# Softplus logs in PSUM, both C products on VectorE each eighth step, and two residual adds moved to TensorE and ScalarE in a Mamba, MoE and attention kernel

## The reference, cut to what matters

```python
# x: (8, 512, 512) f32; every layer adds to the residual
x = x + mamba(layernorm(x))      # L0_attn_a, the scan stage
x = x + moe(layernorm(x))        # 64 experts, top 6 by softmax, and a shared expert
x = x + attention(layernorm(x))
x = x + moe(layernorm(x))

def mamba(x):                    # per batch of 512 positions, 512 channels, 16 states
    xz = einsum('bld,kd->blk', x, W_x)
    dt_raw, b_ssm, c_ssm = xz[..., :128], xz[..., 128:144], xz[..., 144:]
    dt = softplus(einsum('blr,dr->bld', dt_raw, W_dt) + b_dt)
    d_a = exp(dt[..., None] * -exp(A_log))
    dbx = dt[..., None] * b_ssm[:, :, None, :] * x[..., None]
    # h = d_a_t * h + dbx_t;  y_t = sum over the states of h * c_t
    return y + x * D_param
# the shared expert of the MoE layer: silu(h @ sw_gate) * (h @ sw_up) @ sw_down
```

## Time and profile before

| | |
|---|---|
| median of 3 runs | 3007.59 us (3006.03 to 3013.62) |
| profiled execution | 3010.63 us, span 3008.8 us |
| PE, DVE, POOL, ACT busy | 2720.0, 1793.9, 1528.1, 1298.4 us |

### The profile page before, as it was taken

The page is one execution under the profiler, slowest core; times in us unless marked ns, Lnnn a source line. Parts: engine busy times, 40 slices in busy tenths (PEclk is TensorE's granted clock), DMA queues, the critical chain, the costliest instruction groups (busy, mean ns, idle before and its releaser), DMA issues.

```text
span 3008.8 us, 37440 instructions
## 1 busy us (share of the span) xinstructions
PE 2720.0 (90%) x13484; PEld 1436.8 (48%) x13484; DVE 1793.9 (60%) x3787; ACT 1298.4 (43%) x2689; POOL 1528.1 (51%) x944
## 2 busy tenths in 40 slices
PE   4668889988998879999969999999899999999998
PEld 2455555545555534443335555555544444444443
DVE  5899999999999952232246666665524444222222
ACT  4557586766757411111127767666712220111111
POOL 5999999989999902222135555554400001121211
PEclk7769999998999889999989999999999999999999
DMA  5443645546454479999930000001135324899997
GB/s 189 150 168 139 204 168 171 189 136 192 164 192 162 138 295 355 396 394 392 380 109 1 29 29 29 29 29 58 47 100 196 117 74 164 307 383 338 361 334 219
DMA packets 168234, 566.13 MB, mean 188 GB/s; under 512 B 22832, under 2 KB 24752, under 8 KB 167536
## 3 DMA queue, kind: packets, MB, share of 16 engines
q1 hardware_dynamic: 149904, 521.65, 46.7%
q0 software_dynamic: 17088, 40.90, 5.9%
q10 hardware_dynamic: 1056, 1.18, 0.1%
HBM read 487.89 MB, written 75.79 MB: 187 GB/s over the span
## 4 chain that ended last, share of the span: by engine, by line
PE 54%; ACT 2%; DVE 2%; POOL 2%; issue 1%; DMA 1%; POOLq 0%; SPq 0%; DVEq 0%; ACTq 0%
PE bank L1140 10%; PE bank L1166 5%; PE bank L1078 5%; PE bank L1043 5%; PE bank L1064 5%; PE bank L1191 5%; PE bank L1248 4%; PE bank L1225 3%; PE bank L1213 2%; PE bank L1237 2%; POOL arena L1947 2%; PE bank L1123 1%; PE bank L1179 1%; ACT arena L1770 1%; PE bank L1050 1%
## 5 line engine op out<-in xcount | busy, mean ns | idle before, releaser
L1851 POOL TENSOR_TENSOR arena<-arena 128x1024 f32<-128x1024 f32 x256 | 606.3, 2369 | 6.3 <-DMA arena<-scratch_bc 3.0
L1699 ACT ACTIVATE bank<-arena 128x512 f32<-128x512 f32 x512 | 346.6, 689 | 318.9 <-DVE arena L1337 200.5
L1947 POOL TENSOR_TENSOR arena<-arena 128x2048 f32<-128x2048 f32 (+3 forms) x128 | 297.1, 2324 | 275.9 <-DVE arena L1567 275.8
L993 PE MATMUL bank<-arena 128*128 128x128 f32 x2048 | 306.3, 303 | 141.7 <-POOL arena L1857 141.6
L993 PEld LDWEIGHTS bank<-arena 128*128 128x128 f32 x2048 | 260.4, 156 | 227.7 <-POOL arena L1857 181.8
L1770 ACT ACTIVATE arena<-arena 128x256 f32<-128x256 f32 (+3 forms) x512 | 287.2, 566 | 148.9 <-DVE arena L1558 125.2
L1857 POOL TENSOR_TENSOR arena<-arena 128x512 f32<-128x512 f32 x256 | 334.2, 1306 | 21.4 <-DVE arena L1337 21.3
L1337 DVE TENSOR_TENSOR_SCAN arena<-bank,arena 128x512 f32<-128x512 f32 x256 | 310.6, 1213 | 24.8 <-POOL arena L1851 18.6
L1140 PE MATMUL bank<-arena 128*64 128x352 f32 x2048 | 322.7, 468 | 0.0
L1337 DVE TENSOR_TENSOR_SCAN bank<-bank,arena 128x512 f32<-128x512 f32 x256 | 308.4, 1205 | 0.0
L1064 PE MATMUL bank<-arena 128*128 128x512 f32 x640 | 288.3, 593 | 9.1 <-ACT arena L1726 9.1
(11 more groups left out here) (145 smaller groups left out, 4161.3 us busy)
## 6 DMA issues: line engine op xcount, KB each, us to landing
arena<-scratch_bc SPq DMA_DIRECT2D x128, 1024.0 KB, 5.4
arena<-in_w_out SPq DMA_DIRECT2D x128, 768.0 KB, 15.3
arena<-in_w_gate SPq DMA_DIRECT2D x128, 704.0 KB
arena<-in_w_up SPq DMA_DIRECT2D x128, 704.0 KB
scratch_x<-arena SPq DMA_DIRECT2D x16, 1024.0 KB, 4.5
scratch_xn<-arena SPq DMA_DIRECT2D x15, 1024.0 KB, 4.1
arena<-scratch_x SPq DMA_DIRECT2D x44, 256.0 KB, 6.0
arena<-scratch_x SPq DMA_DIRECT2D x8, 1024.0 KB, 7.5
```

The lines of the kernel that those rows point to most:

```text
L993: i = nc.tensor.matmul(y[:, t * P:(t + 1) * P], w[:, n, t * P:(t + 1) * P], p.ident, is_transpose=True, start=False, stop=g == GROUPS - 1 ...
L1699: nc.scalar.activation(bank[p.da_bank(k, n)][:, :], block_of(p.dt, b, c), ACT.Exp, scale=p.alog[:, c, state:state + 1]).then_inc(*p.decaye ...
L1851: nc.gpsimd.tensor_tensor(out=p.hb[k % HB], in0=over(block_of(p.dtx, b, c), 1, NG), in1=p.bc[k // 2 % NBC][:, 0], op=ALU.mult).then_inc(*p ...
L1947: nc.gpsimd.tensor_tensor(out=own, in0=own, in1=over(p.rden[:, k % 2, :], 2, width), op=ALU.mult).then_inc(*p.divided.up(k))
```

## The change

Softplus: `soft_ln` writes the logs of one chunk (128x512) into a bank of the small ring, and `dt_sum` adds them from there, chunk by chunk. Its steps and those of dt are moved forward by one to three. Each eighth step (k % 8 == 4) VectorE leaves the first scan in its bank too and makes both C products, and GpSimd makes none. `y_sum` begins a chunk's bank with identity times x, so that the bank holds the new residual, and `x1` is a copy by ScalarE, three steps behind. For quads 0 to 6 of the first MoE layer the down tile ends with identity times the fetched residual rows, and ScalarE copies it out; the fetch is issued a step earlier. GpSimd's small norm operations (`rstd`) stand a step later.

```diff
+BOTH_EVERY, BOTH_AT = 8, 4
-PREPARE = (("x_in", 4), ("stats_a", 7), ("stats", 8), ("rstd", 8), ("apply", 11))
-TURN_S, DTR, BC, DT = (13, 13, 14, 14), 16, 15, (21, 21, 22, 25)
-SOFT = (("soft_exp", (24, 28)), ("soft_ln", (26, 29)), ("dt_sum", (27, 30)), ("dtx", (28, 31)))
-FRONT = (("stats_a", 1), ("stats", 1), ("rstd", 1), ("apply", 3), ("xn_out", 3), ("gate", 7), ("logit", 9), ("route_max", 10), ("route_exp", 12), ("route1", 13), ("masks", 15))
+PREPARE = (("x_in", 4), ("stats_a", 7), ("stats", 8), ("rstd", 9), ("apply", 11))
+TURN_S, DTR, BC, DT = (13, 13, 14, 14), 16, 15, (19, 19, 20, 22)
+SOFT = (("soft_exp", (24, 27)), ("soft_ln", (25, 28)), ("dt_sum", (26, 29)), ("dtx", (27, 30)))
+BY_BLOCK = ("soft_ln", "dt_sum")
+FRONT = (("stats_a", 1), ("stats", 1), ("rstd", 2), ("apply", 3), ("xn_out", 3), ("gate", 7), ("logit", 9), ("route_max", 10), ("route_exp", 12), ("route1", 13), ("masks", 15))
-X1_BEHIND = 2
+X1_BEHIND = 3
+FETCH_LEAD = 1
+def dve_weighs_both(k):
+    return k % BOTH_EVERY == BOTH_AT
-        yield DOWNS[t], ("fetch", 0, q, t)
+        yield DOWNS[t] - FETCH_LEAD, ("fetch", 0, q, t)
         yield DOWNS[t], ("sd", 0, q, t)
         yield DOWNS[t] + SO_LAG, ("so", 0, q, t)
...
-TAKERS = ("turned", "dtr_out", "bc_out", "dt_out", "logit", "folded", "silu", "hid", "so")
+TAKERS = ("turned", "dtr_out", "bc_out", "dt_out", "dt_sum", "logit", "folded", "silu", "hid", "so")
...
     def y_sum(k):
         b, c, g = step_of(k)
         s, w, each = b % 2, p.hb[k % HB], b * HC + c
@@ -984,11 +1012,17 @@
             PE.wait_ge(p.decay_set)
             if each >= 2:
                 PE.wait_ge(p.x1_added, *divmod(each - 2, HC))
+            wait_x(b)
+            nc.tensor.matmul(y[:, :], p.ident, p.xin[s][:, :, c * P:(c + 1) * P], start=True, stop=False,
+                             skip_group_check=True)
             for t in range(QT):
                 nc.tensor.matmul(y[:, t * P:(t + 1) * P], p.s_xnT[s][:, c, t * P:(t + 1) * P], p.diag[:, c, :],
-                                 start=t == 0, stop=False, skip_group_check=True)
+                                 start=False, stop=False, skip_group_check=True)
         for n, by in enumerate(("pool", "dve")):
-            PE.wait_ge(p.weighted[by], k)
+            if by == "pool" and dve_weighs_both(k):
+                PE.wait_ge(p.weighted_first, k)
+            else:
+                PE.wait_ge(p.weighted[by], k)
             for t in range(QT):
                 i = nc.tensor.matmul(y[:, t * P:(t + 1) * P], w[:, n, t * P:(t + 1) * P], p.ident, is_transpose=True,
                                      start=False, stop=g == GROUPS - 1 and n == NG - 1, skip_group_check=True)
@@ -1079,6 +1113,14 @@
...
+        if p.summed_on_pe(m, q, t):
+            rows, s = last_rows(m, t), (q * QT + t) % OUT[m]
+            nc.tensor.matmul(out[:, :], f["shT"][rows, SC - 1, t * P:(t + 1) * P], f["swd"][rows, SC - 1, :],
+                             start=False, stop=False)
+            PE.wait_ge(p.so_in[s], m, q, t)
+            nc.tensor.matmul(out[:, :], p.ident, f["so"][:, s, :], start=False,
+                             stop=True).then_inc(*ring.made.up("sd", m, q, t))
+            return
...
-    def dt_sum(b, h):
-        V.wait_ge(p.soft_ln, b, h)
-        dt, soft = half_of(p.dt, b, h), half_of(p.dtx, b, h)
-        nc.vector.tensor_tensor(out=dt, in0=dt, in1=soft, op=ALU.add).then_inc(*p.dt_ready.up(b, h))
+    def dt_sum(b, c):
+        ring, dt = p.rings[0], block_of(p.dt, b, c)
+        V.wait_ge(p.soft_ln, b, c)
+        nc.vector.tensor_tensor(out=dt, in0=dt, in1=bank[ring.bank("soft", b, c)][:, :], op=ALU.add).then_inc(
+            *ring.taken_by["dve"].up("soft", b, c))
 
     def scan(k):
         b, c, g = step_of(k)
         h = p.hb[k % HB]
-        banks = [bank[p.da_bank(k, n)] for n in range(NG)]
+        banks, both = [bank[p.da_bank(k, n)] for n in range(NG)], dve_weighs_both(k)
         V.wait_ge(p.fed, k)
         for n in range(NG):
             V.wait_ge(p.decayed, k, n)
-            nc.vector.tensor_tensor_scan(out=banks[n][:, :] if n else h[:, n, :], data0=banks[n][:, :], data1=h[:, n, :],
-                                         initial=0.0, op0=ALU.mult, op1=ALU.add).then_inc(*p.scanned.up(k, n))
+            nc.vector.tensor_tensor_scan(out=banks[n][:, :] if n or both else h[:, n, :], data0=banks[n][:, :],
+                                         data1=h[:, n, :], initial=0.0, op0=ALU.mult, op1=ALU.add).then_inc(
+                *p.scanned.up(k, n))
         V.wait_ge(p.bc_in[k // 2 % NBC], k // 2)
+        if both:
+            V.wait_ge(p.scanned, k, 0)
+            nc.vector.tensor_tensor(out=h[:, 0, :], in0=banks[0][:, :], in1=p.bc[k // 2 % NBC][:, 1, 0, :],
+                                    op=ALU.mult).then_inc(*p.weighted_first.up(k))
         V.wait_ge(p.scanned, k, NG - 1)
         nc.vector.tensor_tensor(out=h[:, NG - 1, :], in0=banks[NG - 1][:, :], in1=p.bc[k // 2 % NBC][:, 1, NG - 1, :],
                                 op=ALU.mult).then_inc(*p.weighted["dve"].up(k))
-
-    def x1(b, c):
-        x = p.xin[b % 2][:, :, c * P:(c + 1) * P]
-        V.wait_ge(p.y_summed, step_at(b, c, GROUPS - 1))
-        nc.vector.tensor_tensor(out=x, in0=x,
-                                in1=bank[Y_BANKS[c % 2]][:, :].rearrange("p (t d) -> p t d", t=QT),
-                                op=ALU.add).then_inc(*p.x1_added.up(b, c))
...
-    def soft_ln(b, h):
-        soft = half_of(p.dtx, b, h)
-        A.wait_ge(p.soft_exp, b, h)
-        nc.scalar.activation(soft, soft, ACT.Ln, bias=1.0).then_inc(*p.soft_ln.up(b, h))
+    def soft_ln(b, c):
+        ring = p.rings[0]
+        A.wait_ge(p.soft_exp, b, c // 2)
+        A.wait_bank(ring, "soft", b, c)
+        nc.scalar.activation(bank[ring.bank("soft", b, c)][:, :], block_of(p.dtx, b, c), ACT.Ln, bias=1.0).then_inc(
+            *p.soft_ln.up(b, c))
...
-        A.wait_ge(p.dt_ready, b, c // 2)
+        A.wait_ge(p.rings[0].taken_by["dve"], "soft", b, c)
         for n in range(NG):
             before, last = divmod(k * NG + n - len(DA_BANKS), NG)
             if before >= 0 and last:
                 A.wait_ge(p.weighted["dve"], before)
+            elif before >= 0 and dve_weighs_both(before):
+                A.wait_ge(p.weighted_first, before)
             elif before >= 0:
                 A.wait_ge(p.scanned, before, last)
             state = g * NG + n
             nc.scalar.activation(bank[p.da_bank(k, n)][:, :], block_of(p.dt, b, c), ACT.Exp,
                                  scale=p.alog[:, c, state:state + 1]).then_inc(*p.decayed.up(k, n))
+
+    def x1(b, c):
+        A.wait_ge(p.y_summed, step_at(b, c, GROUPS - 1))
+        nc.scalar.copy(p.xin[b % 2][:, :, c * P:(c + 1) * P],
+                       bank[Y_BANKS[c % 2]][:, :].rearrange("p (t d) -> p t d", t=QT)).then_inc(*p.x1_added.up(b, c))
...
+    def shared_out(m, q, t):
+        if not p.summed_on_pe(m, q, t):
+            return
+        ring, f = p.ring_with("sd", m, q, t), p.ff[m]
+        A.wait_ge(ring.made, "sd", m, q, t)
+        nc.scalar.copy(f["so"][:, (q * QT + t) % OUT[m], :], bank[ring.bank("sd", m, q, t)][:, :]).then_inc(
+            *ring.taken_by["act"].up("sd", m, q, t))
...
     def weigh_c(k):
+        if dve_weighs_both(k):
+            return
```

More of the change, by code:

```diff
@@ L123, in __init__ @@
         self.index = {k: i for i, k in enumerate(products)}
-        self.made = Signal(prog, name + "_made", products)
+        self.made = Signal(prog, name + "_made", [k for k in products if k[0] != "soft"])
         self.taker = {k: e for k, e in takes}
@@ L285, in first_track @@
     for name, at in FIRST_SOFT:
-        yield at, (name, 0, 1)
+        for key in soft_keys(name, 1):
+            yield at, (name, 0, key)
 def quad_track(q):
@@ L791, in semaphores @@
                 if kind in taken_by:
-                    takes.append(((taken_by[kind][0], *key), taken_by[kind][1]))
+                    product, engine = taken_by[kind]
+                    takes.append(((product, *key), "act" if kind == "so" and self.summed_on_pe(*key) else engine))
                 elif kind == "pcopy":
@@ L818, in semaphores @@
         self.fed = sig("fed", "feed")
-        self.weighted = {"pool": sig("weighted_pool", "weigh_c"), "dve": sig("weighted_dve", "scan")}
+        self.weighted = {"pool": sig("weighted_pool", "weigh_c", where=lambda k: not dve_weighs_both(k)),
+                         "dve": sig("weighted_dve", "scan")}
+        self.weighted_first = sig("weighted_first", "scan", where=dve_weighs_both)
         self.y_summed = sig("y_summed", "sum")
@@ L977, in dt, with wait_x @@
                          start=True, stop=True).then_inc(*ring.made.up("dt", b, c))
+    def wait_x(b):
+        if b > 0:
+            PE.wait_ge(p.x_in[b % 2], b)
+            return
+        for t in range(QT):
+            PE.wait_ge(p.x_first[t], 0)
     def y_sum(k):
```

30 lines of the change are left out of this document (19 added, 11 removed).

## The result

The changed kernel takes 3031.80 us (3025.94 to 3032.81), the kernel before 3008.22 beside it: ratio 1.0079, 95% interval 1.0067 to 1.0091, 24 us slower. Forecast were 2977, 31 us faster. The span is 3029.6 us (before 3008.8).

The account below looks back on a forecast made before the run. VectorE was taken to pace scan batches 2 to 6 and GpSimd batches 0 and 1; −10 (batches 0 and 1), −20 (2 to 6), −2 (batch 7) and +1 behind sum to −31 us, giving 2977, range 2960 to 3001.

Parts of the forecast that it names:

- VectorE's price list: Scan stage, batches 2 to 6: softplus adds −16, x1 and shared experts' adds −12 each, second products +12; sum −28 us.
- Rival 4: Softplus adds keep their price, from another cause than the shared interface: −15 us; counted with rival 1, together 0.20.
- I take 621: Batches 2 to 6 last 621 us, a bit under the middle of TensorE's 613 and 635: −20 us.
- the 36 us of TensorE: Batches 2 to 6: 40 new products with x and the residual at 0.89 us raise TensorE from 577.1 to 612.7.
- I cost it at nothing: Scan stage: ScalarE's new copies (+32 us) and fewer table loads (−15) cost nothing, given 319 us of waits before decays.
- The hope that a busier engine wins part of the low level back: Batches 2 to 6: clock 0.96 means 51 us at the low level, which busier TensorE may win back in part.
- rival 2: Scan stage: TensorE hides all its added work, VectorE's 613 counts; −48 us, 2960; chance 0.13.
- Rival 3: Scan stage: ScalarE's copies wait for TensorE, delay decays and starve VectorE; +14 us, 3021; chance 0.07.
- Rival 1: Batches 2 to 6: TensorE replaces VectorE as pacer, at 99%; −8 to −15 us, about 2998; chance 0.20 with rival 4.
- my own two criteria for being wrong: Scan stage: VectorE's busy time falls by less than 35 us, or new waits over 10 us appear on its queue.

Follow-up runs that it names:

- e17: e14 with the softplus logs in SBUF, added by block, while the ring's turns are still held; 1.0085 of the kernel before, 3036 us.
- e14: e4 with rstd back at steps 8 and 1, logs still in PSUM; 1.0033 of the kernel before.
- e5: The kernel before with only the moved steps of dt, softplus and rstd, logs in SBUF; 1.0049, 3025 us.
- e4: e3 with GpSimd making its C product in every step again; 1.0046 of the kernel before, 3022 us.
- e3: The changed kernel with the x1 and shared experts' adds back on VectorE and the fetch at its old step; 1.0054 of the kernel before, 3025 us.
- e1: The changed kernel with the shared experts' add back on VectorE and the fetch at its old step; 1.0015 of the kernel before, 3013 us.
- e12: The changed kernel with TensorE's residual product kept, but VectorE instead of ScalarE copying the shared experts' sum out; 1.0051 of the kernel before, 3026 us.
- e15: The kernel before with x1 added by TensorE and copied by ScalarE, nothing else; 1.0011, 3011 us.
- e13: The kernel before with dt and softplus at the new steps, rstd at its old ones, logs in SBUF; 1.0035, 3018 us.

## Why the prediction was wrong

**What held.** Batches 0 and 1, on GpSimd: −12 against −10 forecast. VectorE's price list: the new add 0.68 us each, busy 593 in the middle batches against 595. ScalarE's table loads: 95 in the stage instead of 107, the 12 fewer of the forecast. TensorE's: 614.5 against 612.7, its waits for GpSimd's product down to 8.2 (under 15 forecast). That the second SBUF input makes the adds long: the same add by block takes 1832 ns on average from SBUF (e17) and 679 from PSUM (e14), and 677 at its shortest in both. Rival 4 falls by that.

**The step that failed** is "I take 621": that the middle batches last as long as their busiest engine is busy, plus part of its waits. They lasted 666 with TensorE at 614 and VectorE at 593. The measured busy times bear out both engines' sums, and the waits between them do not: two engines near 92 and 89%, coupled by waits in both directions within a step or two, don't overlap for free. Of the miss of 55 us in all (31 faster forecast, 24 slower measured) 45 lie here. The table prices the parts of the change one after another, along e5, e4, e3, e1, e12, after:

| step of the change | us | in the prediction |
|---|---|---|
| moved steps (e5 less before) | +15 | not priced; rstd's move named only for GpSimd |
| logs in PSUM, turns included (e4 less e5) | −1 | −16, turns not priced |
| second product (e3 less e4) | +2 | +12 of VectorE, −5 a batch of GpSimd |
| x1 on TensorE and ScalarE (e1 less e3) | −12 | −12 of VectorE |
| shared experts' residual on TensorE (e12 less e1) | +11 | in the 36 us of TensorE |
| their copy on ScalarE (after less e12) | +8 | "I cost it at nothing" |

They sum to +24, the measured loss, as any such path from before to after must; each but the first is uncertain by 6 to 7 us, so −1 and +2 are nothing. Their order matters: x1 is worth −12, −1.5 or +3 (e15) in different company, and undoing rstd 14 in after. What the sum lacked is thus the moved steps (+15) and the copies (+8), and it took the 16 us that the logs save VectorE for time, which the runs put at 1, give or take 7.

**ScalarE at nothing** failed because its cover, 319 us of waits, was read as a sum. They are spread in front of 509 decays, 0.6 us each; a copy that waits 4.30 us at the head of the queue uses up the share of seven decays at once. The cost itself is shown by e12 against after and by e1's steps 8 to 12. What VectorE's own x1 add waited before (1.1 us) was no bound for it: the shared experts' sum is asked for two steps behind the last product of its tile, and TensorE got 0.89 us more to do exactly there, 1.13 by its line. In VectorE's own queue the 1.1 us were no bound either: with the logs in PSUM that wait was 15.1 (e14).

**The clock** stayed at 0.96 in the middle batches. The hope that a busier engine wins part of the low level back is not borne out here, and rival 2 rested on it. By the Trainium skill (TensorE: Matmul & The Clock Gate, Part 1) activity releases the throttle. Batch 0 agrees, 0.67 with TensorE busy 59% of it, before 0.63 with 55%. Batch 1 rose too, 0.83 from 0.79, with TensorE busy 74% instead of 76, and batch 2 fell from 0.99 to 0.96 with 92% instead of 90, so the busy share alone doesn't forecast it here.

**Rivals.** Rival 3 (slower, 3021) had the right sign and, for a part of the loss, the right chain, with 7 in 100. Rival 2 fell with the clock and the time. Rival 1 was not it either: TensorE is 92% busy in the middle batches, not 99. Rival 3 expected the x1 copies at the batch halves; it was rather the shared experts' copies, and they are a third of the loss. Of my own two criteria for being wrong one was met: the waits on VectorE's queue grew by far more than 10 us. The other was not: its busy time fell by 51 us as it should (1793.9 to 1742.6). Why dt and softplus cost 10.5 us at their new steps (e13) isn't settled: no single wait in its trace has that size, and that trace is of an execution as fast as the kernel before (3010.66 us), so it can't show the loss.

## What to carry to other kernels

When an edit also moves steps of a schedule, run the moves alone first: here they cost 15 us before any instruction got cheaper. When it takes turns of a shared ring, look for the place where the ring's producer becomes the later engine: what is saved in front of it is only waited out there. A us saved on the engine that paces a stage is worth its full length only while the other engines' slack at that very place is longer than the wait that the edit puts into their queues; average slack is no cover for an in-order queue. Before moving an add to "idle" engines, look at what stands right behind it in the new queue. And compare the unchanged instructions of two traces too: here one of them made 8 us of difference.

## What the runs showed of the hardware

- A two-input add of 128x512 f32 on VectorE beside a busy GpSimd took 1832 ns on average with both inputs in SBUF (30 times, e17; 677 to 8072 ns) and 679 with one in PSUM (675 to 686 in after). Cutting the SBUF add into halves made it dearer in sum (53.8 us against 42.5): as if each instruction paid its own standstill.
- Such a standstill can outlast several GpSimd instructions: the routing product of 128x256 in e14 stood through four in a row (6.40 us, shortest 0.43).
- The stage's clock rose with TensorE's load from batch 0 to 2 (0.67, 0.83, 0.96), but 37 us more work in the middle five left it at 0.96.
